# Eight row buffers in the slot loop, one shared batch started earlier, and the last norm per batch on ScalarE

## The reference

```
x = layernorm(x + attention(x))        # layer 0: one head, W_qkv and W_out
x = layernorm(x + experts0(x))         # 8 experts 128 -> 512 -> 128, SiLU, best 2 by softmax of their
                                       # logits, and a shared expert over all tokens
x = layernorm(x + state_space(x))      # layer 1: rmsnorm, projection to 2 x 256, causal convolution
                                       # of 4 taps, SiLU, low-rank step size with softplus, a scan with
                                       # 16 states per channel, gate, projection back to 128;
                                       # its own residual is added inside
x = layernorm(x + experts1(x))         # the same with gated experts: (silu(x wg) * (x wu)) wd
```

## Time and profile before

| | |
|---|---|
| median of three runs | 783.93 us |
| the profiled execution | 779.94 us |
| its span | 778.2 us |
| TensorE matmul busy | 585.1 us (75%) |
| VectorE busy | 427.5 us (55%) |
| ScalarE busy | 328.1 us (42%) |
| GpSimd busy | 353.5 us (45%) |

### The profile page before, as it was taken

The page is one execution under the profiler, slowest core; times in us unless marked ns, Lnnn a source line. Parts: engine busy times, 40 slices in busy tenths (PEclk is TensorE's granted clock), DMA queues, the critical chain, the costliest instruction groups (busy, mean ns, idle before and its releaser), DMA issues.

```text
span 778.2 us, 9134 instructions
## 1 busy us (share of the span) xinstructions
PE 585.1 (75%) x2522; PEld 345.9 (44%) x2523; DVE 427.5 (55%) x725; ACT 328.1 (42%) x578; POOL 353.5 (45%) x279
## 2 busy tenths in 40 slices
PE   6886897878785738849777895575588899999930
PEld 4754575555553313314323341231344666666620
DVE  2345561000012669999999999998257333332336
ACT  3433334434443365763874674342122244434410
POOL 1001225566652306685677666566100356555423
PEclk9998799999998669999997987989799999999975
DMA  3513001111113933433443343342000111111131
GB/s 108 170 36 123 14 13 36 38 39 40 37 33 89 390 113 136 135 125 136 137 151 117 127 164 108 108 157 73 14 1 1 24 35 41 35 36 34 33 112 55
DMA packets 35133, 65.58 MB, mean 84 GB/s; under 512 B 6111, under 2 KB 23207, under 8 KB 34464
## 3 DMA queue, kind: packets, MB, share of 16 engines
q1 hardware_dynamic: 29824, 51.19, 19.6%
q0 software_dynamic: 4992, 9.32, 4.6%
q10 hardware_dynamic: 288, 4.72, 1.6%
HBM read 57.60 MB, written 8.52 MB: 85 GB/s over the span
## 4 chain that ended last, share of the span: by engine, by line
PE 43%; issue 15%; DVE 15%; POOL 11%; ACT 8%; another core or an unknown queue 4%; DMA 2%; POOLq 1%; SPq 0%; DVEq 0%; ACTq 0%
PE ps L597 8%; PE ps L578 8%; DVE wide L1333 7%; POOL wide L1454 5%; PE ps L580 4%; POOL w L1454 4%; PE ps L532 4%; PE ps L589 4%; ACT work L926 3%; PE ps L690 2%; PE ps L518 2%; PE ps L522 2%; PE ps L523 2%; PE ps L632 1%
## 5 line engine op out<-in xcount | busy, mean ns | idle before, releaser
L1333 DVE TENSOR_TENSOR_SCAN wide<-work,ps 128x1024 f32<-128x1024 f32 x64 | 146.2, 2284 | 3.6 <-ACT work L926 1.8
L926 ACT ACTIVATE work<-work,a_neg 128x512 f32<-128x512 f32 (+1 forms) x128 | 84.5, 712 | 105.6 <-DVE wide L1333 85.3
L1477 POOL DMA_INDIRECT xin<-xn_rows,source x78 | 76.1, 975 | 110.2 <-DVE dest L1150 76.6
L1483 POOL DMA_INDIRECT y_choice<-yout,dest x78 | 78.9, 1012 | 86.6 <-ACT yout L753 62.7
L1454 POOL TENSOR_TENSOR wide<-wide,w 128x1024 f32<-128x1024 f32 x32 | 75.5, 2361 | 70.0 <-DVE wide L1333 70.0
L690 PE MATMUL ps<-w,ident 128*128 128x512 f32 x128 | 70.6, 685 | 28.5 <-POOL w L1454 28.5
L1454 POOL TENSOR_TENSOR w<-wide,w 128x1024 f32<-128x1024 f32 x32 | 77.4, 2422 | 32.1 <-DVE wide L1333 32.1
L1175 DVE COPY xT<-ps 128x128 f32<-128x128 f32 x78 | 22.7, 291 | 120.3 <-PE ps L572 68.5
L690 PE MATMUL ps<-wide,ident 128*128 128x512 f32 x128 | 65.7, 637 | 26.2 <-POOL wide L1454 26.2
L1326 DVE TENSOR_TENSOR ps<-ps,w 128x1024 f32<-128x1024 f32 x64 | 78.9, 1233 | 7.1 <-DVE wide L1333 0.9
L1180 DVE TENSOR_TENSOR wide<-wide,ps 128x512 f32<-128x512 f32 x39 | 26.8, 688 | 75.3 <-ACT wide L818 56.6
(11 more groups left out here) (231 smaller groups left out, 928.4 us busy)
## 6 DMA issues: line engine op xcount, KB each, us to landing
w<-bc_rows SPq DMA_DIRECT2D x64, 512.0 KB, 3.6
w<-in_w ACTq DMA_DIRECT2D x2, 2304.0 KB, 9.0
w<-y_choice SPq DMA_DIRECT2D x16, 256.0 KB, 3.6
wg<-in_wg SPq DMA_DIRECT2D x1, 2304.0 KB, 10.4
wu<-in_wu SPq DMA_DIRECT2D x1, 2304.0 KB, 15.4
wd<-in_wd SPq DMA_DIRECT2D x1, 2304.0 KB, 20.4
xin<-xn_rows,source POOLq DMA_INDIRECT x78
y_choice<-yout,dest POOLq DMA_INDIRECT x78
```

What stands on the lines that cost most here:

```text
L926: last = A(dA[j % 2][:, h, lo:S], delta[:, h, lo:S], ACT.Exp, scale=a_neg[:, j + h * NS:j + h * NS + 1])
L1333: V.tensor_tensor_scan(st[j % 2].rearrange("p h t -> p (h t)"), dA[j % 2].rearrange("p h t -> p (h t)"), dbu.rearrange("p h t -> p (h t)") ...
L1477: G.indirect_dma_start(out=xin[i % 4][:, :], out_offset=None, in_=xn_rows, in_offset=bass.IndirectOffsetOnAxis(ap=source[:, i:i + 1], axis ...
L1483: G.indirect_dma_start(out=y_choice, out_offset=bass.IndirectOffsetOnAxis(ap=dest[:, y:y + 1], axis=0), in_=yout[y % 4][:, :], in_offset=N ...
```

## The change

Four edits:

1. The ring of row buffers grows from four to eight (the four new ones lie in `normed`, an array that is not in use then). A gather waits for the transpose of slot i - 8, and the scatter after gather i is that of slot i - 8. The output buffers remain four. The loop body has eight steps and runs 4 times; the steps written out around it are the same in number.
2. Layer 0's norm of batches 1 to 3 stands before `hand_over` and `weigh_input` on VectorE. VectorE's seven copies and fills of small constants move from the end of attention to the start of the program.
3. In layer 1, `shared_up`, `shared_silu` and `shared_mult` of batch 0 stand ahead of `turn_normed(3)` on TensorE, ahead of `apply_norm(3)` on ScalarE (with the load of the table for SiLU), and after `add_residual(3)` on VectorE. In both layers `counts` stands after the first two blocks of shared batch 1, and VectorE's pieces of `routing` have the products of batches 1 to 3 between them at new places.
4. In the tail each batch is a group of its own. ScalarE normalises it (`last_norm`), with a scale from GpSimd's power, of one row instead of two, and a shift that VectorE makes (`pull_mean`).

```diff
+RING = 8
-        xin = [sb(f"xin{k}", [P, D]) for k in range(4)]
+        xin = [sb(f"xin{k}", [P, D]) for k in range(4)] + [normed[:, k, :] for k in range(4)]
...
-        LOOP_TRIPS = (ROUTED - 2 - LOOP_LO) // 4
+        LOOP_TRIPS = (ROUTED - 2 - LOOP_LO) // RING
...
-                for k in range(4):
+                for k in range(RING):
                     step(m, LOOP_LO + k)
...
-        GROUPS = (((0, 1), (1, NB)), ((0, NB // 2), (NB // 2, NB)))
+        GROUPS = (((0, 1), (1, NB)), tuple((b, b + 1) for b in range(NB)))
@@ TensorE, moe
-                shared_up(0)
                 if l == 0:
-                    shared_up(1)
-                    counts()
-                else:
-                    counts()
-                    shared_up(1)
+                    shared_up(0, 0)
+                shared_up(l, 1, (0, 1))
+                counts()
+                shared_up(l, 1, (2, 3))
                 shared_down(0)
@@ TensorE, end of the state-space stage
             project_out(NB - 1)
+            pe.wait_ge(ld_f1, 48)
+            shared_up(1, 0)
             turn_normed(NB - 1)
@@ ScalarE
+            def last_norm(b):
+                act.wait_ge(pull_set, b + 2)
+                for t in range(b * QT, b * QT + QT):
+                    last = A(x_tile(t), tile_of(base[1], t), ACT.Identity, bias=pull[:, t:t + 1], scale=inv2[:, 0, t:t + 1])
+                last.then_inc(layer_out[1].sem, 1)
...
+            act.preload_act_table(ACT.Silu)
+            shared_silu(1, 0)
             apply_norm(NB - 1)
             router(1, NB - 1, LOOSE[0])
             moe(1)
+            for b in range(NB):
+                last_norm(b)
@@ VectorE, moe: pieces of the routing and products of the shared expert
+                go_on(3)
+                mult(1, 0, 1)
+                go_on(3)
+                mult(1, 2, 3)
                 go_on()
-                shared_mult(0, 0, 1)
-                go_on()
-                shared_mult(0, 2, 3)
-                go_on(4)
-                shared_mult(1, 0, 1)
-                go_on()
-                shared_mult(1, 2, 3)
@@ VectorE, tail
                         combine(l, b)
-                        if b == NB // 2 - 1:
-                            variances(l, 0)
-                        if b == NB // 2:
-                            norm_group(l, 0)
-                    variances(l, 1)
-                    norm_group(l, 1)
+                        variances(l, b)
+                        if b:
+                            pull_mean(l, b - 1)
+                    pull_mean(l, NB - 1)
...
+            def pull_mean(l, g):
+                first, end = GROUPS[l][g]
+                own = slice(first * QT, end * QT)
+                dve.wait_ge(*std_set[l].at(g + 1))
+                V.scalar_tensor_tensor(out=pull[:, own], in0=all_mv[:, own, 0], scalar=-1.0, in1=inv2[:, 1 - l, own],
+                                       op0=ALU.mult, op1=ALU.mult).then_inc(pull_set, 1)
@@ VectorE, between layer 0's experts and the states
             variances(0, 1)
+            norm_group(0, 1)
             hand_over(0)
             weigh_input(0)
-            norm_group(0, 1)
             for b in range(NB):
                 states(b)
             gate_sum(NB - 1)
             add_residual(NB - 1)
+            shared_mult(0, *range(HB))
             take_logits(1, NB - 1, LOOSE[1])
             moe(1)
@@ GpSimd
-                for i in range(ROUTED + 7):
+                for i in range(ROUTED + RING):
                     if i < ROUTED:
-                        if i >= 4:
-                            pool.wait_ge(*x_ps[l].at(i - 3))
-                        G.indirect_dma_start(out=xin[i % 4][:, :], out_offset=None, in_=xn_rows,
+                        if i >= RING:
+                            pool.wait_ge(*x_ps[l].at(i - RING + 1))
+                        G.indirect_dma_start(out=xin[i % RING][:, :], out_offset=None, in_=xn_rows,
...
-                    if i >= 7:
-                        y = i - 7
+                    if i >= RING:
+                        y = i - RING
                         pool.wait_ge(*yout_set[l].at(y + 1))
```

More of the change, by code:

```diff
@@ L273, in build @@
         sy_ps = layers("sy_ps", NB); base_set = layers("base_set", NB)
-        xin_loaded_ = [layers(f"xin_loaded{k}", 16 * fills(k)) for k in range(4)]
+        xin_loaded_ = [layers(f"xin_loaded{k}", 16 * fetches(k)) for k in range(RING)]
         xin_loaded = [[r[l] for r in xin_loaded_] for l in range(2)]
@@ L487, in _, with shared_up @@
             router(0, NB - 1)
+            def shared_up(l, b, blocks=range(HB)):
+                pe.wait_ge(*nT_set[l].at(b + 1))
+                for j in blocks:
+                    n = b * HB + j
+                    own = slice(NE * HID + j * P, NE * HID + (j + 1) * P)
+                    if l == 0:
+                        if b > 0:
+                            pe.wait_ge(*sT_set[0].at(n - HB + 1))
+                        mm_(bank(4 + j), w1[:, own], nT_all[:, b * S:(b + 1) * S], start=True, stop=True).then_inc(sh_ps[0].sem, 1)
+                    else:
+                        if n >= 2:
+                            pe.wait_ge(*sT_set[1].at(n - 1))
+                        mm_(bank(4 + j % 2), wg[:, own], nT_all[:, b * S:(b + 1) * S], start=True, stop=True)
+                        mm_(bank(6 + j % 2), wu[:, own], nT_all[:, b * S:(b + 1) * S], start=True, stop=True)\
+                            .then_inc(sh_ps[1].sem, 1)
             def moe(l):
@@ L799, in _, with shared_silu @@
             router(0, NB - 1)
+            def shared_silu(l, b):
+                for j in range(HB):
+                    n = b * HB + j
+                    act.wait_ge(*sh_ps[l].at(n + 1))
+                    if l == 0:
+                        if b >= 2:
+                            act.wait_ge(*sy_ps[0].at(b - 1))
+                        A(sT[b % 2][:, j, :], bank(4 + j), ACT.Silu).then_inc(sT_set[0].sem, 1)
+                    else:
+                        if n >= 2:
+                            act.wait_ge(*sT_set[1].at(n - 1))
+                        A(th[j % 2], bank(4 + j % 2), ACT.Silu).then_inc(gate_set[1].sem, 1)
             def moe(l):
@@ L1211, in moe @@
                 go_on(2)
-                shared_mult(2, 0, 1)
+                mult(2, 0, 1)
                 go_on()
@@ L1490, in _ @@
             moe(1)
-            for g in range(2):
+            for g in range(NB):
                 inverse_group(1, g)
```

106 lines of the change are left out of this document (41 added, 65 removed).

## The result

The changed kernel took 769.48 us (median of 4 runs, 765.71 to 770.54), the kernel before 782.7 on the same chip (4 runs). The ratio is 0.985, with a 95% interval of 0.981 to 0.990: 13 us less where 13.9 were forecast. The profiled execution took 768.80 us, its span 767.1 against 778.2: 11.1 less. I read those 11.1 from timelines, as intervals between events that both kernels have. The last interval ends with the last normalisation; the store behind it takes 3.0 us in both.

What follows compares the result with a forecast made beforehand. No one engine bounds the kernel; TensorE leads in turns, and layer 0's loop waits at the output side. -1.5 - 0.6 - 3.4 - 5.5 - 2.9 = -13.9 from the 783.93 median gives 770.0 us; own range 765 to 775, wider 752 to 777.

Steps and rivals of the forecast that it cites:

- (a): Slot loops, eight row buffers: waits at the output side stay; layer 0 -1.5 us, layer 1 -0.6.
- 0.5 us in (a) for expert registers: Layer 0's slot loop: fewer loop turns, fewer expert registers loaded cold, 0.5 us gained.
- Rival A: Layer 0's loop: the gathers were the brake, so it falls to GpSimd's own pace; 744.3 us, chance 0.10.
- my sign of being wrong: Slot loops: the forecast is wrong if layer 0's or 1's loop changes by more than 3 us either way.
- Rival B: Layer 1's slot loop: freed gathers never slip late, so its stalls go; 761.6 us, chance 0.15.
- (b): Layer 0's norm of batches 1 to 3 moves into VectorE's idle time before the first state's product: -3.4 us.
- (c): Layer 1's head: shared batch 0 fills TensorE's idle time after the last projection, counts come earlier: -5.5 us.
- rival C: Layer 1's head: TensorE's clock drops inside the newly placed shared blocks; 772.8 us, chance 0.12.
- the rest of the head is TensorE in order with one stall for VectorE that moves along: Layer 1's head after batch 1: the gain, 6.5 us before the allowance for the clock, carries through.
- (d): Tail: ScalarE's norm per batch, fewer VectorE steps and a smaller power before the end: -2.9 us.
- Rival D: Slot loops: the eight-step body does not stay in TensorE's instruction store; 795 to 800 us, slower, chance 0.06.

Runs made afterwards that it cites:

- e7_noring: The changed kernel without its first edit: four row buffers, body of four steps, scatter 7 behind; median 745.94 us, ratio 0.990 to the kernel before.

## Why the forecast held, and which of its steps did not

**(a), the row buffers: wrong in its reading, and in sign for layer 1.** I read the stall in the earlier trace rows as a wait at the output side: four output buffers, each freed by a scatter four slots earlier. The trace of the kernel before contradicts that already. The late output copy at 164.37 is that of slot 12, and the scatter of slot 8 had started at 151.45, 12.9 us earlier. No copy of layer 0 starts less than 6.9 us after the scatter that frees its buffer, and where the landing of scatters is on record (the kernel before on the third chip) it comes 2.3 us after issue (median), and each copy starts at least 4.6 us after its buffer was free. Beside the late copy stands another late row, VectorE's copy of transposed rows, which waits for TensorE alone and for no output buffer:

```profile
161.52 0.27 PE L572 MATMUL ps<-ident,xin 128*128 128x128 f32 x1
...
164.41 0.29 DVE L1175 COPY xT<-ps 128x128 f32<-128x128 f32 x1 [5.44 <-remote]
```

The same kernel without stalls, on the third chip:

```profile
163.06 0.27 PE L572 MATMUL ps<-ident,xin 128*128 128x128 f32 x1
...
163.37 0.29 DVE L1175 COPY xT<-ps 128x128 f32<-128x128 f32 x1 [2.01 <-PE ps L572]
```

That is 2.62 us after the transpose's end against 0.04. The trace's record of semaphore updates, which no view prints, has the updates for this transpose and for the product ahead of it, which TensorE ended at 161.79 and 161.69, at 164.30 and 164.26. In the six profiles with stalls this copy is over 1 us late for 9 to 11 of layer 0's 39 slots, up to 3.8 us; in the other eight it is never over 0.21. So the stall in the loop is of the same kind as the late sum above: the engines hear late of TensorE's work, and GpSimd waits for them. What delays the news is open. That it is GpSimd's indirect transfers, 1.25 to 1.3 us apart, is argued, not shown: for it speak nine gathers against four, and that rows whose release the profile ties to no work of the core (`remote`) stand in the two slot loops and nowhere else; but one transfer a slot, and eight output buffers, never ran where there are stalls.

Layer 0's loop gained 2.1 us, near the 1.5 forecast, but on that kind of chip the four profiles with four buffers lie between 120.22 and 123.28 us and the two with eight at 119.48 and 121.16, so this agreement says little. In layer 1, -0.6 was forecast; +2.57 to the first scatter and -0.24 behind it came. I had counted four more gathers at the start as free because they lie beside other work. They were the burst, and it accounts for 1.37 of the 2.57 us, up to the first transpose. The other 1.20 lie behind it, where TensorE's granted clock in the next 9 us was 0.62 (604 to 613) against 0.81 before (613 to 622); the kernel with the row buffers alone has the same late transpose, but 0.81 there and only 0.3 us of it. The 0.5 us in (a) for expert registers had no row, and no run shows it by itself.

Rival A (GpSimd's own pace) was given 744.3 and "the gathers were the brake" as its cause. Its pace is real on the second and third chip: with four row buffers a slot takes 2.6 us there (98.0 us from first to last scatter), and eight buffers take off 5.45 us in all. So there the row buffers were part of the brake, and my sign of being wrong, a loop that changes by more than 3 us, came true. What made the 2.1 us where there are stalls isn't shown. The medians of e7_noring and the changed kernel are 9.0 us apart; the profiles show 5.45 of it, and the rest is not located (e7_noring's profile is the fastest of its six runs, the changed kernel's the slowest).

Rival B (layer 1's stalls go) fell: 121.85 us from first to last scatter before, 121.61 after, and 117.5 on the other chips with either number of buffers. Its price was too high as well. Of the 135 us I had given about 3 to filling and emptying the loop and 9 to stalls; from the first transpose (612.87) to the first scatter (625.35) alone, the work of the first slot included, it is 12.5, and the stalls are the 4.4 between 121.85 and 117.48.

**(b), the norm: right.** Forecast -3.4. The five profiles without it have 36.97 to 38.33 from combine to product, the nine with it 33.76 to 34.65. The 2.72 us that VectorE still waits before L1313 are the slack that the step counted on.

**(c), the head of layer 1: mechanism right, size off.** ScalarE's norm comes 9.45 us after the projection's start instead of 6.20, 3.25 later where 3.5 was forecast, and the four blocks run at full clock. The sum gave 6.5 before I took 1.0 off for the clock. At the start of batch 2's second half the gain was 5.27 us (589.13 - 549.08 against 577.16 - 542.38): 1.2 had been lost at half clock behind the new blocks. The eight router products took 1.88 us where I had them 0.9 shorter, and the blocks of batch 1 held the counts: VectorE's mask was ready 3.8 us earlier, the counts began only 2.5 earlier, where 4.3 was forecast. In the kernel with the head alone the router products took 1.06, and nothing was lost there (its 4.8 are 6.5 - 1.7). Behind that point another 1.7 were lost. TensorE's four pairs of products of the second half of batch 2 took 5.23 us (577.16 to 582.39) instead of 3.54 (589.13 to 592.67), for the granted clock was lower after nearly the same idle time (2.13 and 2.08 us). The window of the kernel before, then that of the changed kernel:

```profile
588.00:594.00 6.00, 4.87 (x20) 2.96 (x21) 6.00 (x6) 1.20 (x2) 0.00 (x0) 1.00 0.00 0
```

```profile
576.00:582.00 6.00, 4.84 (x8) 2.07 (x9) 6.00 (x6) 0.60 (x1) 0.00 (x0) 0.72 0.01 3
```

This is no chance: the four pairs take 5.23 or 5.24 us in all nine profiles with edit 3, on every chip, and 3.54 in all five without. So rival C had the right cause, the granted clock, in the wrong place: the 2.9 us lost to it bring 6.5 to 3.6, between my 5.5 and its 2.7. The term that was mis-sized is "the rest of the head is TensorE in order with one stall for VectorE that moves along": the stall moved along, TensorE's clock behind it did not.

**(d), the tail: right.** -3.2 for -2.9, the same in every kernel with the edit (24.61 to 24.98 against 27.91 to 27.99 us); no table load stands before the Identity norms.

**Not forecast.** From the first to the last scan came 3.1 us that no step had. The edits don't decide that interval: 249.2 us with the norm alone and with the head alone, 252.25 with the tail alone, and the changed kernel had 249.21 once and 251.71 the second time. The ten profiles with 251.06 to 252.37 all have one wait of VectorE of 1.4 us for ScalarE's exponentials, the four with 249.2 to 249.3 have none. The kernel before had it both times (252.29 and 252.37), so that the change has no part in it isn't shown either. The first gather of layer 0, 1.25 us later, goes with TensorE's clock in 83.5 to 90 us:

```profile
83.50:90.00 6.50, 6.41 (x8) 2.73 (x9) 3.65 (x14) 1.79 (x3) 1.77 (x3) 0.52 0.01 3
```

It was 0.72 before. Over the fourteen profiles the two go together, from 0.97 with the first gather at 107.72 to 0.50 at 112.43. The kernel with eight output buffers had its first gather at 112.12 in one profile and at 110.81 in the other, so some of this is chance too.

The 1.14 us from there to layer 0's first scatter go with the clock too, and not with the burst. The kernel before, then the changed kernel:

```profile
118.00:128.00 10.00, 8.68 (x45) 5.64 (x46) 1.75 (x6) 4.41 (x9) 5.61 (x6) 1.00 0.17 35
```

```profile
118.00:128.00 10.00, 7.75 (x29) 4.45 (x30) 2.64 (x9) 3.15 (x6) 4.16 (x5) 0.83 0.16 35
```

The eight profiles with 0.83 in this window have 15.85 to 16.10 us between the two events, the six with 1.00 have 14.60 to 14.96, and either group has kernels with four and with eight buffers.

So the agreement of the sum, 13.2 us for 13.9 in medians and 11.1 in the profiles, is in part luck: what (a) and (c) didn't bring was paid for by the scans, which no step had.

**Rival D** (longer loop body): the instruction queue moved 15 packets instead of 14, and layer 1's loop with the body of eight took 117.50 us against 117.48 with four on the second chip. By the rule of the Trainium skill, "Runtime: NRT & Kernel Launch", section "Instruction fetch mechanics", the body fits, and these rows agree.

## What to carry to other kernels

Check a forecast by its terms and not by its sum: here five intervals were off by 1 to 3 us each in a sum of 14, and the errors partly cancelled. A wait that the profile puts down to an unknown source is not evidence for the buffer that would fit it. Look when that buffer was last used, and look beside it for a wait that has no buffer: both stood in the first trace. When transfers are issued earlier because buffers are free, count what every other engine is waiting for at that moment.

## What was not expected of the hardware

The same kernel took 782.7 and 774.0 us on two occasions and 753.2 and 752.2 on two others. The difference between the two kinds lies in the slot loops: 103.88 against 123.28 us in layer 0 from first scatter to combine, 117.48 against 121.85 in layer 1 between first and last scatter. TensorE's granted clock over the span was the same 0.909 in both profiles. In layer 0's loop with stalls VectorE's copy of the transposed rows, which waits for TensorE alone, started up to 3.8 us after TensorE's end; without stalls never more than 0.21 us after it. And 2.1 us of idle time before the same products were followed by full clock in one kernel and by 0.72 of it (576 to 582 us) in the other, with the same 3.54 and 5.23 us for the products on every chip.
